# Inverse roots of the first graph stage: one 16-column GpSimd power instruction in place of VectorE's two iterations

## The reference, cut to what matters

```python
x = x + gnn0(layernorm(x), adj)      # the stage of this change
x = x + ffn0(layernorm(x))           # top 2 of 8 experts by token
x = x + gnn1(layernorm(x), adj)
x = x + ffn1(layernorm(x))

# gnn0, for each of 32 batches of 256 nodes, 4 heads of 32
X, q, k = lrelu(h @ W_lin + b), lrelu(h @ W_q), lrelu(h @ W_k)
adj_h = adj * sigmoid(q k^T * scale)
deg = sum(adj_h, axis=-1)
dis = where(deg > 0, deg ** -0.5, 0)
Y = (dis * adj_h * dis^T) @ X
out = (Y - mean(Y)) * rsqrt(var(Y) + eps) * ln_g + ln_b
```

## Time and profile before

| what | us |
|---|---|
| median of 3 runs | 715.95 |
| lowest and highest of them | 713.38, 718.05 |
| span of the profiled execution | 714.2 |
| first graph stage, start to the last send | 0 to about 306 |
| slots 2 to 31 of it | 33 to about 261 |

### The profile page before, as it was taken

One profiled execution on the slowest core, in us unless ns is written; L12 is line 12 of the kernel. 1 busy time (PEld: TensorE's weight loads), 2 busy tenths in 40 slices (PEclk: granted clock), 3 DMA queues, 4 the chain that ended last, 5 costly groups with the idle time before them and its releaser, 6 DMA issues. The chain is left out here.

```text
span 714.2 us, 18526 instructions
## 1 busy us (share of the span) xinstructions
PE 624.0 (87%) x5412; PEld 525.6 (74%) x5412; DVE 526.9 (74%) x2348; ACT 469.6 (66%) x1284; POOL 345.6 (48%) x520
## 2 busy tenths in 40 slices
PE   3788998888889978679999999996789879999993
PEld 2455666556556646669999999996788767999993
DVE  8799999999999978734444444443899951678898
ACT  2778988988888843237676676672257767666661
POOL 1024534766666666724554554545443105755540
PEclk9999999999999989989999999998999979999998
DMA  5329232233232110546543455324894101022122
GB/s 159 104 85 212 77 104 75 93 112 118 75 91 83 46 46 31 167 123 168 137 123 116 137 151 146 101 58 111 183 257 131 60 1 61 11 80 61 30 61 59
DMA packets 75828, 72.15 MB, mean 101 GB/s; under 512 B 7777, under 2 KB 64802, under 8 KB 74962
## 3 DMA queue, kind: packets, MB, share of 16 engines
q1 hardware_dynamic: 61938, 50.28, 25.5%
q0 software_dynamic: 11200, 13.35, 7.7%
q10 hardware_dynamic: 2592, 7.34, 3.6%
HBM read 44.39 MB, written 26.55 MB: 99 GB/s over the span
## 5 line engine op out<-in xcount | busy, mean ns | idle before, releaser
L1515 ACT ACTIVATE hT<-psum,b1blk 128x128 f32<-128x128 f32 x364 | 104.1, 369 | 53.4 <-PE psum L1452 53.4
L1628 POOL DMA_INDIRECT expert_outputs<-y_rows,y_at x91 | 87.5, 962 | 96.6 <-DVE y_rows L1601 93.1
L1452 PE MATMUL psum<-xinT,w1blk 128*128 128x128 f32 x728 | 97.8, 278 | 0.2 <-ACT xinT L1505 0.2
L1473 PE MATMUL psum<-f_w,hT 128*128 x728 | 96.4, 276 | 0.0
L1452 PEld LDWEIGHTS psum<-xinT,w1blk 128*128 128x128 f32 x728 | 89.8, 194 | 0.8 <-ACT xinT L1505 0.5
L1473 PEld LDWEIGHTS psum<-f_w,hT 128*128 128x128 f32 x728 | 88.4, 192 | 0.2
L1582 DVE TENSOR_SCALAR w1blk<-f_w 128x256 f32 x182 | 47.1, 300 | 46.4 <-issue 43.5
L836 DVE TENSOR_TENSOR adj_h<-psum,adjT 128x1024 f32<-128x1024 f32 x64 | 75.2, 1215 | 0.6 <-ACT psum L612 0.6
L612 ACT ACTIVATE psum<-psum 128x1024 f32<-128x1024 f32 x64 | 64.1, 1007 | 15.3 <-PE psum L362 15.3
L1167 POOL DMA_INDIRECT pair_rows<-rows,row_of x64 | 63.4, 990 | 17.2 <-issue 15.9
L1601 DVE TENSOR_TENSOR y_rows<-psum,b2wide 128x128 f32<-128x128 f32 x91 | 26.6, 292 | 52.8 <-PE psum L1473 47.5
(11 more groups left out here) (324 smaller groups left out, 1475.4 us busy)
## 6 DMA issues: line engine op xcount, KB each, us to landing
adj_in<-in_adj_dram SPq DMA_DIRECT2D x32, 256.0 KB, 3.7
adjT_scratch<-adjT SPq DMA_DIRECT2D x32, 256.0 KB, 3.0
adjT<-adjT_scratch SPq DMA_DIRECT2D x6, 1024.0 KB, 5.2
xin<-pair_rows SPq DMA_DIRECT2D x91, 64.5 KB, 1.9
b2wide<-b_of_blocks ACTq DMA_DIRECT2D x10, 512.0 KB
xres<-in_x_dram SPq DMA_DIRECT2D x16, 256.0 KB, 3.7
xres<-expert_outputs POOLq DMA_DIRECT2D x6, 512.0 KB, 8.2
out_dram<-yout SPq DMA_DIRECT2D x6, 512.0 KB, 3.2
```

The costliest lines, as they stand in the source:

```text
L1452: ins = nc.tensor.matmul(psum[:, 2 + u, lo:lo + P], w1blk[:, u, k, c * P:(c + 1) * P], xinT[:, u, :], start=True, stop=True)
L1473: ins = nc.tensor.matmul(psum[:, 6 + n % 2, 0:D], hT[:, u, k, c, :], flat[:, bass.ds(places[k] + (HID + c * D), D)], start=(k == 0 and c = ...
L1515: ins = nc.scalar.activation(hT[:, u, k, c, :], psum[:, 2 + u, lo:lo + P], ACT.Gelu, bias=b1blk[:, c, k, n:n + 1])
L1628: pool.indirect_dma_start(y_dram[:, :], bass.IndirectOffsetOnAxis(ap=y_at[:, n % Y_AT:n % Y_AT + 1], axis=0), y_rows[:, u, :], None).then_ ...
```

## The change

In the slots 1 to 31 GpSimd itself makes `veps` and the inverse roots; VectorE keeps only `dis` and `shift`. The slots outside keep the iterations. GpSimd's share of a slot goes from five small instructions to seven and one power instruction on 16 columns (`pow` with an exponent tile of -0.5). It squares half the difference of the means where VectorE had multiplied by a factor, so the scale `STRETCH` goes out of the numbers of these slots. The waits that guard `rstd` against being overwritten (`sets_read`) move to GpSimd with it. VectorE waits for the result at the end of the slot, behind `take_degrees`, where before it waited for the sums near the start.

```diff
-        SUMS = 5
+        SUMS = 8
@@ solve_steps (VectorE)
                 if 0 < s < NB:
                     assert stats_by(s - 1) == stats_upto[s - 1]
-                    yield
-                    dve.wait_ge(s_sums, SUMS * s - 1)
-                else:
-                    dve.wait_ge(s_stats, stats_upto[s - 1])
+                    for _ in range(11):
+                        yield
+                    dve.wait_ge(s_sums, SUMS * s)
+                    nc.vector.scalar_tensor_tensor(dis[:, s % SETS, :], v[:, NLN:NLN + NDEG], DEG_MIN,
+                                                   r[:, NLN:NLN + NDEG], ALU.is_gt, ALU.mult).then_inc(s_norm, 1)
+                    nc.vector.scalar_tensor_tensor(shift[:, s % SETS, :], msum[:, :], -0.5, r[:, 0:NLN],
+                                                   ALU.mult, ALU.mult).then_inc(s_norm, 1)
+                    return
+                dve.wait_ge(s_stats, stats_upto[s - 1])
...
@@ take_degrees (VectorE)
-                nc.vector.tensor_scalar(veps[:, b % 2, NLN:NLN + NDEG], heads_of(Y_BANK)[:, :, 0], DEG_MIN, STRETCH,
-                                        ALU.max, ALU.mult).then_inc(s_degmax, 1)
+                nc.vector.tensor_scalar(veps[:, b % 2, NLN:NLN + NDEG], heads_of(Y_BANK)[:, :, 0], DEG_MIN,
+                                        STRETCH if b + 1 == L0 else 1.0, ALU.max, ALU.mult).then_inc(s_degmax, 1)
@@ sums_of_stats (GpSimd)
                 nc.gpsimd.tensor_tensor(mdiff[:, :], mean_a, mean_b, ALU.subtract).then_inc(s_sums, 1)
                 nc.gpsimd.tensor_tensor(sqsum[:, :], sq_a, sq_b, ALU.add).then_inc(s_sums, 1)
                 pool.wait_ge(s_sums, SUMS * (s - 1) + 1)
+                nc.gpsimd.tensor_scalar(mdiff[:, :], mdiff[:, :], 0.5, None, ALU.mult).then_inc(s_sums, 1)
+                pool.wait_ge(s_sums, SUMS * (s - 1) + 2)
+                nc.gpsimd.tensor_scalar(sqsum[:, :], sqsum[:, :], 1.0 / D, EPS, ALU.mult, ALU.add).then_inc(s_sums, 1)
+                pool.wait_ge(s_sums, SUMS * (s - 1) + 3)
                 nc.gpsimd.tensor_tensor(mdiff[:, :], mdiff[:, :], mdiff[:, :], ALU.mult).then_inc(s_sums, 1)
-                pool.wait_ge(s_sums, SUMS * (s - 1) + 2)
-                nc.gpsimd.tensor_scalar(sqsum[:, :], sqsum[:, :], STRETCH / D, STRETCH * EPS, ALU.mult, ALU.add)\
-                    .then_inc(s_sums, 1)
                 nc.gpsimd.tensor_tensor(msum[:, :], mean_a, mean_b, ALU.add).then_inc(s_sums, 1)
+                pool.wait_ge(s_sums, SUMS * (s - 1) + 5)
+                nc.gpsimd.tensor_tensor(v[:, 0:NLN], mdiff[:, :], sqsum[:, :], ALU.add).then_inc(s_sums, 1)
+                pool.wait_ge(s_degmax, s)
+                sets_read(pool, s)
+                pool.wait_ge(s_sums, SUMS * (s - 1) + 7)
+                nc.gpsimd.tensor_tensor(rstd[:, s % SETS, :], v, minus_half[:, :], ALU.pow).then_inc(s_sums, 1)
```

More of the change, by code:

```diff
@@ L115, in build_program @@
         CONST2 = 7
-        CONST2_ALL = CONST2 + 2 * (NE - 1) + 2
+        CONST2_ALL = CONST2 + 2 * (NE - 1) + 3
         rows_dram = nc.dram_tensor("pair_rows", (NPAIR * STRIDE + NPAIR * P, ROW), F32).ap()
@@ L225, in build_program @@
         newt = sb1("newt", [P, NLN + NDEG])
+        minus_half = sb1("minus_half", [P, NLN + NDEG])
         guess = sb1("guess", [P, NLN + NDEG])
@@ L294, in ranks, with sets_read @@
             return None
+        def sets_read(engine, s):
+            if batch(s - 6):
+                engine.wait_ge(s_yn, s - 5)
+            if batch(s + 1):
+                engine.wait_ge(s_xh, s + 2)
+            if batch(s - 8):
+                engine.wait_ge(s_xh1, s - 7)
         def gnn0_sync(sp):
@@ L767, in solve_steps @@
                     dve.wait_ge(s_norm, 2 * solve_no(s) - 2)
[L768 to L778, removed]
+                chA.mark(nc.vector.tensor_tensor(msum[:, :], mean_a, mean_b, ALU.add))
+                chA.mark(nc.vector.tensor_tensor(mdiff[:, :], mean_a, mean_b, ALU.subtract))
+                chA.mark(nc.vector.tensor_tensor(sqsum[:, :], sq_a, sq_b, ALU.add))
+                yield
+                chA.settle()
+                chA.mark(nc.vector.tensor_tensor(mdiff[:, :], mdiff[:, :], mdiff[:, :], ALU.mult))
+                chA.mark(nc.vector.tensor_scalar(sqsum[:, :], sqsum[:, :], STRETCH / D, STRETCH * EPS,
+                                                 ALU.mult, ALU.add))
+                yield
+                chA.settle()
                 chA.mark(nc.vector.scalar_tensor_tensor(v[:, 0:NLN], mdiff[:, :], 0.25 * STRETCH, sqsum[:, :],
@@ L805, in solve_steps @@
                 chA.settle()
[L806 to L811, removed]
+                sets_read(dve, s)
                 chA.mark(nc.vector.scalar_tensor_tensor(r, newt[:, :], 5.0, guess[:, :], ALU.add, ALU.mult))
@@ L816, in solve_steps @@
                                                r[:, NLN:NLN + NDEG], ALU.is_gt, ALU.mult).then_inc(s_norm, 1)
-                if 0 < s < NB:
-                    dve.wait_ge(s_sums, SUMS * s)
                 nc.vector.scalar_tensor_tensor(shift[:, s % SETS, :], msum[:, :], -0.5, r[:, 0:NLN],
@@ L1126, in gnn0_gpsimd @@
         def gnn0_gpsimd(pool):
+            nc.gpsimd.memset(minus_half[:, :], -0.5).then_inc(s_const2, 1)
+            pool.wait_ge(s_const2, CONST2_ALL)
             pool.wait_ge(s_wln, 2 * 16)
@@ L1150, in sums_of_stats @@
                 mean_a, sq_a, mean_b, sq_b = (stats[:, was, :, i] for i in (1, 2, 4, 5))
+                v = veps[:, was, :]
                 pool.wait_ge(s_stats, stats_by(s - 1))
```

## The result

The changed kernel takes 751.4 us (median of 4 runs, 748.7 to 752.7), where the kernel before took 715.2 us (4 runs, 713.4 to 718.1) beside it: a ratio of 1.050, 95% interval 1.046 to 1.053. It is 36 us slower. The forecast was 715 us, within a range of 709 to 733; the time lies above the range.

The account below looks back on a forecast made before the run. TensorE and ScalarE were taken to set the slots, GpSimd those from 14 to 29; +1.3 there, +0.4, -0.5, start -0.8 and end -1.2 gave -0.8 us on 715.95, about 715.0 us, range 709 to 733.

Parts of the forecast that it names:

- How long the power takes: Length of GpSimd's power instruction on 16 columns, shown by no row: taken as 1.0 us, between 0.22 and 2.5.
- What bounds the kernel: Plain slots are set by TensorE and ScalarE at 7.27 us; VectorE, 95% full, runs beside them with little slack.
- The ceiling of 0.9 us in four late slots: All that a faster VectorE can give in the later slots: about 0.9 us in four slots.
- Room on GpSimd: GpSimd's wait for shift, 5.7 us in four late slots, less 2.0 for added instructions: 0.92 us for one power.
- X: Length of one power instruction on GpSimd in us, taken as 1.0.
- the term for the slots 14 to 29: These slots are bound by GpSimd: 4 groups x 4 x (1.0 - 0.92) = +1.3 us.
- In the slots before 14 there are no sends and X may be far longer without harm.: Slots before 14: dis needs the power only at the slot's end, about 5 us after GpSimd can have it.
- The late `shift`: dis, shift after the degrees: 0 to 0.1 us a slot; as rival, 0.3 in 28 slots, 723 us, chance 0.05.
- The edges: Start and end of the stretch of slots 1 to 31: -0.8 us at the start, -1.2 us at the end.
- The sum: Terms +1.3, +0.4, -0.5, -0.8, -1.2: together -0.8 us, about 715.0 us; 16 us for each us of power.
- rival 2: The power is dear: GpSimd bounds the slots from 14 on; at 2.0 us +17.3, 733 us; chance 0.28.
- VectorE's busy time: Nine instructions fewer in each of 31 slots, 1.5 us a slot: busy time falls by about 47 us.

Follow-up runs that it names:

- the run with the unread power: Kernel before plus one power instruction on 16 constant columns after GpSimd's sums in slots 1 to 31, result never read: 748.7 us, ratio 1.048.
- the early `shift`: Changed kernel with a product of constants for the power, and dis and shift ahead of taking the degrees: ratio 0.995; again 706.7 us, 0.987.
- The runs with constants: Changed kernel with the power replaced by a plain product of constants on the same 16 columns: 708.2 us, 0.990; again 709.9 us, 0.992.
- the first and third set: Sets of four runs, each set on one chip beside the kernel before, which took 715.8 us in the first and 715.2 us in the third.
- the run with 8 columns: Changed kernel with the power on the 8 variance columns and a product of constants on the 8 degree columns: 727.5 us, ratio 1.016.
- the second set: Set of four runs on one chip, where the kernel before, run beside them, took 731.4 us.
- the power on 4 columns: Changed kernel with the power on the first 4 columns only, the other 12 keeping old values: 733.3 us against 731.4, ratio 1.003.

## Why the prediction was wrong

The step that failed is "How long the power takes": 1.0 us, with an upper end of 2.5 us, where the row shows 2.93 us. With an instruction of 0.22 us in its place the whole loss of 36 us is gone. The upper end was built from nine plain instructions in a row, as if a power were as much arithmetic as the iterations that it replaces, and the value was taken from the indirect send, the only other long software row of GpSimd. Neither row says anything of a power, and the true cost lay outside both ends. The range was closed at a power of 2.0 us, so the time fell out of it.
Point by point:

- *What bounds the kernel.* Right. TensorE and ScalarE set the plain slot. With nine instructions a slot gone from VectorE and the power short, the slot was 7.27 us as before. VectorE stood close behind them: the run with the unread power, which made its instructions 0.56 us a slot longer, made the slot 0.5 us longer. The ceiling of 0.9 us in four late slots for VectorE's relief was set too low, 1.3 us were reached with the early `shift`. The runs with constants won 5 to 9 us in all on the chips of the first and third set, a good part of it outside the steady slots.
- *Room on GpSimd.* The mechanism is right, the size was too small. By the prediction's terms a late slot has (31.27 - 5.7) / 4 + 0.5 = 6.9 us of other work on GpSimd and with the power 9.8 us; measured are 9.61 on average. With X = 2.93 the term for the slots 14 to 29 is 16 x (2.93 - 0.92) = +32.2 us. Measured are +28.0 in slots 14 to 30, or 1.65 us a slot, which leaves a room of 2.93 - 1.65 = 1.28 us and not 0.92; the run with 8 columns gives 1.27 (1.89 less 10.4 / 17). Part of the difference is that the first late slots were nearly as short as before (7.57 and 7.72 us in slots 14 and 15) though GpSimd's sums were already 9.9 and 9.6 us apart: it can fall behind for a while before anyone waits.
- *"In the slots before 14 there are no sends and X may be far longer without harm."* Wrong somewhere between 1.9 us (8 columns and a product, no loss in the slots 5 to 12) and 2.93. I counted the way from the sums to `dis` and left out that the additions stand behind the power and that VectorE's row statistics wait for them ahead of `dis`. It cost 4.1 us in slots 5 to 13, and with the additions first it was gone.
- *The late `shift`.* 0 to 0.1 us a slot was taken, 3.2 us in all were measured between two runs with constants. The size is right for the sum over the slots, with up to 1 us of it put down to the clock in slot 1; the place is not, since plain slots pay nothing and the slots with a ranking and behind it pay 0.2 to 0.3 us. On the chip of the second set it may cost more, see the power on 4 columns.
- *The edges.* With X = 2.93 the prediction's terms give +2.9 us at the end, measured +4.0; at the start -0.8, measured -0.8.
- *The sum.* The prediction's own formula, with the measured length put in, gives +32.2 + 0.4 - 0.5 - 0.8 + 2.9 = +34.2 us. The span grew by 35.0. That this is so near is luck in part: the late slots came out 4.2 us below their term, and the slots 5 to 13, for which the sum had next to nothing, 4.1 us above. Its shape, no effect of VectorE's relief and 16 us for each us of the power beyond 0.92, was that of rival 2, which had 0.28, and was right in its mechanism and too short in its length. The mis-sized length carries nearly the whole error of the forecast.
- *VectorE's busy time* fell by 20 us, not by 47. The records of neighbouring instructions overlap, so nine instructions of 170 ns do not fill 1.5 us: in the slots 5 to 13 of the third set, with the power against the iterations, VectorE's busy time falls from 64.6 to 55.0 us, 1.07 us a slot or 33 in 31 slots. With constants it fell by 26 us in all (526.9 to 500.8). What makes up the rest was not looked into.

## What to carry to other kernels

Before a function is moved to GpSimd in a loop that is full elsewhere, measure that one instruction: an operation that no row shows can't be bounded by its neighbours, and a power here costs some 75 times a plain instruction per column. Then count two things on the engine that receives it: the sum of its work in a slot against the slot, and what stands behind the new instruction in its order, since the same power cost 11 to 12 us less once the additions went ahead of it. Look too at what the receiving engine's work will now run beside: one of VectorE's instructions took 0.59 us beside a GpSimd addition instead of 0.17. A busy share of 95% was no proof that VectorE bound the slot; the waits of TensorE said better what its relief was worth, though a little too low.

## What the runs showed of the hardware

TensorE's clock fell in single slots of the changed kernel. Two slots in the windows (columns as in the earlier trace rows; the granted clock is the third value from the end):

```profile
169.29:178.42 9.13, 6.86 (x73) 4.41 (x72) 7.27 (x24) 6.72 (x14) 8.14 (x14) 1.00 0.34 99
178.42:191.63 13.21, 10.14 (x74) 5.90 (x73) 8.77 (x25) 6.72 (x14) 11.90 (x18) 0.66 0.30 85
```

In slot 20 TensorE had waited 2.48 us for `xd` (183.72 us), the granted clock of the slot is 0.66 where it is 1.00 in the slot before, so part of it ran at the lower of the two levels (1.2 instead of 2.4 GHz), and the output matmuls (L434) took 1.94 us instead of 1.07. The stretches of the late slots and of the drain, after and before:

```profile
core 0: us, PE busy (x) PEld busy (x) DVE busy (x) ACT busy (x) POOL busy (x), PEclk, DMA share, GB/s
125.00:284.40 159.40, 127.69 (x1238) 81.65 (x1238) 118.35 (x359) 112.38 (x238) 141.37 (x217) 0.94 0.23 71
284.40:341.00 56.60, 42.24 (x307) 33.37 (x306) 40.03 (x199) 17.87 (x43) 45.66 (x53) 0.81 0.25 74
```

```profile
121.60:253.00 131.40, 118.32 (x1239) 79.33 (x1238) 125.92 (x507) 111.24 (x238) 89.40 (x170) 1.00 0.28 86
253.00:306.00 53.00, 39.55 (x311) 30.20 (x310) 42.14 (x217) 17.70 (x43) 37.27 (x45) 0.90 0.27 80
```

In the late slots GpSimd waits only once for VectorE (0.4 us), so the slower matmuls hardly delayed it; no run separated the clock. In the drain the clock is 0.81 against 0.90, and 2.7 us more of TensorE's busy time stand in it (42.24 against 39.55); how much of the +4.0 us of that part is the clock was not separated.

One chip differs from the others. On it the same program took 731.4 us instead of 715 us. The plain slots were the same 7.27 us, but from slot 15 on ScalarE's copy of the transposed rows came late behind its matmul, and TensorE waited for the copy of the degrees behind it. The waits from 143 to 238 us in the kernel with the power in slots 1 to 13, which runs VectorE's iterations there, first on that chip, then on the chip of the third set:

```profile
ACT xh1T L662 <- PE psum L500: 15.7, 12, 1.5
...
PE psum L525 <- ACT deg L668: 6.0, 9, 0.7
```

```profile
ACT xh1T L662 <- PE psum L500: 6.1, 12, 1.2
```

The same wait is 15.7 us in 12 times on one chip and 6.1 us on the other. But the late slots hold only a part of the difference. The two profiles differ by 18.9 us (729.8 and 710.9): 4.6 us in slots 14 to 30 (136.6 against 132.0), 11.7 from slot 31 to the last send (61.9 against 50.2, at a granted clock of 0.75 against 0.90), 3.7 behind the last send, and -1.1 in slots 0 to 4, where slot 1 is at the lower clock on the chip of the third set. What makes it stays open. A gain of a few us in these parts can hide in it, so it is best told on one chip.
